# Graph passes: GpSimd's scratch memsets go, and a wait in mid-group comes in

## The chip, the cores and the metric

The kernel runs on one core of a Trainium2 chip. A core has TensorE (PE: matrix products; "PEld" are its weight loads), VectorE (DVE), ScalarE (ACT), GpSimd (POOL) and SyncE (SP, which here issues DMAs and posts semaphores). They run side by side and wait for each other by semaphores. The metric is the device time in microseconds (us) of one execution, as the median of several.

## What is computed

One graph of 6250 nodes (256 features each) and 206,250 edges sorted by destination is used twice:

```python
edge_index = jnp.stack([src, dst])
x = x + _L0_gnn_ref(_layernorm(x), edge_index, ...)   # graph attention, 4 heads: softmax over each node's edges, weighted sum of rows h[src]
x = x + _L0_ffn_ref(_layernorm(x)[None], ...)[0]      # 8 experts, top 2
x = x + _L1_gnn_ref(_layernorm(x), src, dst, edge_weight, ...)  # sum of edge_weight * row[src] per dst, then dense layers
x = x + _L1_ffn_ref(_layernorm(x)[None], ...)[0]      # attention on a second graph of 131,072 edges picks among 4 experts
```

The change touches the two passes over the 206,250 edges: "attention" (first line, tag g0) and "weighted" (third line, tag g1).

## The kernel before, in words

Both passes are built by `graph_pass`. Edges come in tiles of 128. A tile's source rows are fetched from a table in HBM by one indirect DMA of GpSimd (a gather, one row per partition). A one-hot matrix of the tile's destinations within a block of 128 nodes is made by VectorE, and TensorE multiplies the two: the product is the tile's sum per node, which VectorE adds to the block's row of `acc` in SBUF. There are 49 node blocks. A tile whose edges straddle two blocks is used once for each, so TensorE and VectorE go through `NS` = 1664 slots.

Eight tiles are a group (`GRP` = 8, `HG` = 4 is half of it), and the gathered rows lie in a ring of four groups (`RINGS` = 4). GpSimd's instructions run in order. Before each group it waits until the place in the ring is free.

Attention (`step_attending`, 208 groups k, gathers at L834): the wait ahead of group k is for TensorE's sums of group k-4 (`summed(k - RINGS, PAIRS - 1)` on the semaphore "part"). VectorE's step for a group needs all its 8 gathers (L996 is the first instruction that reads them), scales the rows (L990), and adds the sums of the group before (L953). TensorE's sums are L1124. From group 107 on VectorE also ranks the edges of the second graph (a scan L906 and a predicated copy L912 in every second group). After the last group GpSimd issues 16 scatters of that ranking (`tail`, L618).

Weighted (`step_placing`, 202 groups g of 8 gathers at L845, since each tile is fetched once): TensorE goes by 208 steps of 8 slots (L1156), each in two halves of 4 slots, and each half posts the semaphore "sum". VectorE adds them at L961 and makes the one-hots at L941. Because of the doubled tiles, TensorE's slot of a tile is later than the tile's own number by the number b of its node block (0 to 48). A step of TensorE waits until every group that it reads has landed whole (ScalarE posts that at L1050), so a step that reads the end of group g-2 and the start of group g-1 runs after the last gather of g-1 has landed. How far the sums are in terms of gathered groups comes from a table (`tables.summed(g)`): SyncE waits at L822 for the half that holds the last tile of group g and then raises the semaphore "room" by one. GpSimd waits ahead of group g for room of g - AHEAD + 1 with `AHEAD` = 3, which is the sums of group g-3. In the last 130 groups one scatter (L618) follows each group's gathers. A later pass over the second graph (tag q, gathers at L1699) has the same loop without memsets.

In both passes GpSimd clears a part of a scratch tile IDLE after every second gather (L838, L849). Nothing reads it.

Of the kernel before, what the change touches and what calls it, by code (L numbers as in the profile page):

```python
# [33 lines left out]
P = 128  # L34
# [20 lines left out]
TG = NTE // GRP  # L55
AHEAD = 3
# [90 lines left out]
def at_least(eng, sem, value):  # L147

    if not isinstance(value, int) or value > 0:
        eng.wait_ge(sem, value)  # L150
# [544 lines left out]
def graph_pass(sh, tag, planned, planned_block, table, width, acc, acc_zeroed, gather_done, rounds0, keep=None, gmax=None,  # L695
# [10 lines left out]
    RND = SG // RINGS  # L706
    HG = GRP // 2
    BANKS = 4
    names = ["loaded", "onehot", "added", "idle"]
    if attend:  # L710
        names += ["iota", "part", "copied", "z", "lr", "arg", "p", "pcol", "gp"]
    else:
# [3 lines left out]
    s = {n: sh.sem(f"{tag}_{n}") for n in names}  # L716
    with Scope(nc) as sc:
# [13 lines left out]
        WT = sc.sb(f"{tag}_WT", [P, NS]) if not attend else None  # L731
        G = sc.sb(f"{tag}_G", [P, RINGS, GRP, width])
        S = sc.sb(f"{tag}_S", [P, RINGS, GRP, P])
        IDLE = sc.sb(f"{tag}_IDLE", [P, HG, 32])
        if attend:
            pM = [sc.ps(f"{tag}_pM{j}", [P, 512]) for j in range(BANKS)]
        else:
# [1 line left out]
        if attend:  # L739
            ST = sc.sb(f"{tag}_ST", [P, GRP, P])  # L740
            PAIRS = GRP // 2
# [58 lines left out]
        def summed(k, pair):  # L800
            return k * PAIRS + 5 + pair
# [5 lines left out]
        @block.sync  # L807
        def _(sp):
            sp.dma_start(IDX[:, :], planned[0] if attend else src_tiles).then_inc(s["loaded"], 16)
            sp.dma_start(REL[:, :], planned[1]).then_inc(s["loaded"], 16)  # L810
            if attend:
                sp.dma_start(BLK[:, :], planned_block).then_inc(s["loaded"], 16)
            if ranking:
                sp.dma_start(DST, sort.dst_t).then_inc(s["loaded"], 16)
                sp.dma_start(SRC, sort.src_t).then_inc(s["loaded"], 16)
            if not attend:
                sp.dma_start(WT[:, :], planned[2]).then_inc(s["loaded"], 16)

                with sp.Fori(0, TG - AHEAD) as g:
                    sums = sp.value_load(tables.summed(g), min_val=1, max_val=2 * SG)  # L820
                    sp.wait_ge(s["sum"], sums)
                    sp.sem_inc(s["room"], 1)  # L822

        @block.gpsimd
        def _(pool):
            pool.wait_ge(s["loaded"], n_loads)

            def step_attending(k):

                r = k % RINGS  # L830
                if k >= RINGS:
                    pool.wait_ge(s["part"], summed(k - RINGS, PAIRS - 1))
                for u in range(GRP):
                    pool.indirect_dma_start(G[:, r, u, :], None, table, bass.IndirectOffsetOnAxis(  # L834
                        ap=IDX[:, k * GRP + u:k * GRP + u + 1].bitcast(U32), axis=0)).then_inc(gather_done[r], 16)
                    if u % 2 == 1:
                        at_least(pool, s["idle"], (k - 1) * HG + u // 2 + 1)
                        pool.memset(IDLE[:, u // 2, :], 0.0).then_inc(s["idle"], 1)  # L838

            def step_placing(g):  # L840

                r = g % RINGS
                at_least(pool, s["room"], g - AHEAD + 1)
                for u in range(GRP):
                    pool.indirect_dma_start(G[:, r, u, :], None, table, bass.IndirectOffsetOnAxis(  # L845
                        ap=IDX[:, g * GRP + u:g * GRP + u + 1].bitcast(U32), axis=0)).then_inc(gather_done[r], 16)
                    if u % 2 == 1:
                        at_least(pool, s["idle"], (g - 1) * HG + u // 2 + 1)
                        pool.memset(IDLE[:, u // 2, :], 0.0).then_inc(s["idle"], 1)  # L849
                if g >= TG - place:  # L850
                    sort.place(pool, 1)

            if attend:
                pool.iota(RANK, [[P, NTF]], base=P * NTS, channel_multiplier=1,
                          allow_small_or_imprecise_dtypes=True).then_inc(s["rank0"], 1)
                for k in range(SG):
                    step_attending(k)
                pool.wait_ge(s["prep"], 7)
                pool.wait_ge(s["addr"], 4)
                sort.place(pool, tail)  # L860
            else:
                for g in range(TG):
                    step_placing(g)
                sort.place(pool, tail)
# [1700 lines left out]
def build(nc, a, out):  # L2565
# [3 lines left out]
    with ExitStack() as ctx:  # L2569
# [23 lines left out]
        with Scope(nc) as layer:  # L2593
            keep = layer.sb("keep0", [P, NB, 2 * HEADS])
            gmax = layer.sb("gmax0", [P, HEADS])
            acc = layer.sb("acc0", [P, NB, D + HEADS])
            project_nodes(sh, "p0", stats, a["L0_gnn_W"], D + 2 * HEADS, att=(a["L0_gnn_att_src"], a["L0_gnn_att_dst"]),
                          table=table0, table_cols=D + HEADS, keep=keep, keep_from=D, zero=(acc, acc_zeroed[0]), clear=slots)
            table_maximum(sh, "m0", keep, 0, gmax)
            graph_pass(sh, "g0", planned, planned_block, table0, D + HEADS, acc, (acc_zeroed[0], NB), gather_done, 0,  # L2600
                       keep=keep, gmax=gmax, sort=sort, tail=16)
            finish_attention(sh, "f0", acc, table0, keep, gmax, a["L0_gnn_bias"], a["x"], sort, 60)
# [4 lines left out]
        with Scope(nc) as layer:  # L2607
            weights = layer.sb("weights0", [P, TOP, NB])
            pos = layer.sb("pos0", [P, TOP, NB], I32)
            pos_get = layer.sb("pos_get0", [P, TOP, NB], I32)  # L2610
            expert_of = layer.sb("expert_of0", [1, NT_MAX], I32)
            node_of = layer.sb("node_of0", [P, NT_MAX], I32)
            ew_scope = Scope(nc)
            ew = ExpertWeights(sh, ew_scope.__enter__(), "ew0", 8, 1024, a["L0_ffn_W1"], a["L0_ffn_b1"],
                               a["L0_ffn_W2"], a["L0_ffn_b2"], ln_g=a["L0_ffn_ln_g"], ln_b=a["L0_ffn_ln_b"])
            with Scope(nc) as inner:
                stats2 = inner.sb("stats2", [P, NB, 2])
                with Scope(nc) as router:
                    logits = router.sb("logits0", [P, NB, 8])
                    project_nodes(sh, "p1", stats, a["L0_ffn_Wr"], 8, keep=logits, stats2=stats2, sort=sort, count=37, fetch=ew.fetch)  # L2620
                    add_bias(sh, "rb", logits, a["L0_ffn_br"], 8)
                    second_stats(sh, "s2", stats2)
                    route(sh, "r0", 8, logits, weights, pos, pos_get, expert_of, sort, 20)
                order_rows(sh, "t0", 8, stats, stats2, pos, node_of, rows[0], ew, sort, 45)
            experts(sh, "e0", 8, 1024, ew, expert_of, node_of, rows[0], ys, y_stored, sort, 5)
            ew_scope.ctx.close()
            acc = layer.sb("acc1", [P, NB, D])
            tables = TileTables(sh, layer, "tt", planned_block, a["first_dst"], graph_rounds)
            combine(sh, "c0", weights, pos_get, ys, y_stored, (16 * ((tiles_of(8) + 1) // 2), 16 * (tiles_of(8) // 2)),
                    then=(stats, table1, acc, acc_zeroed[1], tables), sort=sort, scatters=10)  # L2630
            sh.end_layer()


            graph_pass(sh, "g1", planned, planned_block, table1, D, acc, (acc_zeroed[1], 1), gather_done, graph_rounds,
                       sort=sort, place=130, tail=8, src_tiles=a["src_t"], tables=tables)
            finish_weighted(sh, "f1", acc, stats, a["L1_gnn_W1t"], a["L1_gnn_W2t"], a["L1_gnn_b1"], a["L1_gnn_b2"], sort, 93)
# [84 lines left out]
```

## Time and profile before

| what | us |
|---|---|
| median of 3 runs (7681.4 to 7688.64) | 7682.64 |
| the profiled execution, its own time | 7684.64 |
| its span from first to last instruction | 7682.9 |
| GpSimd busy in the span | 5707.3 (74%) |
| TensorE busy | 5447.3 (71%) |
| VectorE busy | 3924.1 (51%) |
| ScalarE busy | 1568.1 (20%) |

The span is one line of time for the whole kernel. The attention pass lies at about 195 to 2344 us and the weighted pass at about 3650 to 5864 us. A busy share is a mean over all stages, so each stage is to be read by its own waits. Times of single instructions come from one profiled execution, a matmul's end is modelled, and a wait is put down to the event that came last before it ended.

### The profile page before, as it was taken

Reading aid. Unit: us, or ns where it says so; the run is one execution under the profiler, and the core shown is the slowest. Engines: PE = TensorE matmul, PEld = TensorE weight load, DVE = VectorE, ACT = ScalarE, POOL = GpSimd, SP = SyncE. Lnnn points to the kernel's source line nnn. Section 1 sums busy time; section 2 is a strip of 40 time slices with the busy share of each in tenths; the row PEclk is TensorE's granted clock in tenths of the full one; section 3 lists DMA queues with packets and bytes.
Section 4 is the critical chain, followed back from the end, with each engine's and each line's share of the span. In section 5 each row is a group of like instructions: output and inputs, shape, how many; then the busy total and the mean of one; then the engine's idle time right before and its main releaser. Section 6 shows DMA issues by size and latency. Waiting matters only on the chain. (4 is left out here: it accounts for less than half of the span.)

```text
span 7682.9 us, 117784 instructions
## 1 busy us (share of the span) xinstructions
PE 5447.3 (71%) x27644; PEld 4598.9 (60%) x27645; DVE 3924.1 (51%) x10109; ACT 1568.1 (20%) x3440; POOL 5707.3 (74%) x7330
## 2 busy tenths in 40 slices
PE   3888888777772599990555555555556589999993
PEld 3666666666661489880444434344435589999983
DVE  4777777888887500005454544444445533333326
ACT  1222222222220233330000000000001234444431
POOL 2888888888876577776888888888886577777762
PEclk7888888888885699995777777776777678888886
DMA  3333333333333255553333333333331133333698
GB/s 121 106 106 106 106 107 105 103 103 103 102 101 95 85 174 174 171 172 117 104 104 104 102 92 92 92 92 92 92 93 49 28 86 79 80 79 80 71 72 188
DMA packets 426071, 793.43 MB, mean 103 GB/s; under 512 B 129162, under 2 KB 267134, under 8 KB 425684
## 3 DMA queue, kind: packets, MB, share of 16 engines
q0 software_dynamic: 235504, 474.87, 26.8%
q1 hardware_dynamic: 190436, 317.20, 12.2%
q14 instruction: 97, 0.79, 0.0%
q8 instruction: 34, 0.56, 0.0%
HBM read 720.67 MB, written 70.98 MB: 103 GB/s over the span
## 5 line engine op out<-in xcount | busy, mean ns | idle before, releaser
L1156 PE MATMUL g_pM<-g_G,g_S 128*128 x3328 | 1196.6, 537 | 1190.0 <-ACTq L1050 1070.9
L834 POOL DMA_INDIRECT g_G<-table,X x1664 | 1611.4, 968 | 401.9 <-issue 385.6
L845 POOL DMA_INDIRECT g_G<-table,g_IDX x1616 | 1542.1, 954 | 416.7 <-issue 392.3
L1156 PEld LDWEIGHTS g_pM<-g_G,g_S 128*128 128x128 f32 x3328 | 916.0, 282 | 1470.5 <-issue 1272.4
L1124 PE MATMUL g_pM<-g_G,g_S 128*128 128x260 f32 x3328 | 1125.3, 481 | 407.5 <-DVE acc L953 400.6
L618 POOL DMA_INDIRECT slots<-sort_PAIR,sort_ADDR x1024 | 1029.1, 1005 | 415.4 <-issue 276.2
L1699 POOL DMA_INDIRECT q_G<-table,slot x1072 | 1028.3, 959 | 370.3 <-issue 320.6
L961 DVE TENSOR_TENSOR acc<-g_pM,acc 128x256 f32 x1664 | 698.4, 420 | 1005.4 <-PE g_pM L1156 1002.6
L1124 PEld LDWEIGHTS g_pM<-g_G,g_S 128*128 128x128 f32 x3328 | 706.5, 231 | 692.7 <-DVE acc L953 566.5
L953 DVE TENSOR_TENSOR acc<-g_pM,acc 128x260 f32 x1664 | 711.2, 427 | 188.8 <-PE g_pM L1124 40.4
L941 DVE TENSOR_SCALAR g_S<-iota,g_REL,g_WT 128x128 f32<-128x128 f32 x1664 | 591.2, 356 | 193.2 <-issue 172.4
L990 DVE TENSOR_TENSOR g_G<-g_G,g_pF 128x512 f32<-128x512 f32 x832 | 546.7, 678 | 0.3 <-ACT g_pF L1073 0.3
L1360 ACT ACTIVATE f_XT<-f_pT 128x512 f32<-128x512 f32 x49 | 28.8, 597 | 2329.2 <-PE f_pT L1373 2329.2
L1486 PE MATMUL q_pH<-ew_XT,ew_W 128*128 (+1 forms) x3136 | 489.3, 321 | 0.0
L1486 PEld LDWEIGHTS q_pH<-ew_XT,ew_W 128*128 128x128 f32 x3136 | 462.6, 232 | 3.3
L1114 PEld LDWEIGHTS g_pA<-keep,g_ST 128*128 128x128 f32 x3328 | 407.8, 197 | 78.3 <-issue 71.4
L2356 DVE TENSOR_TENSOR e_Y<-e_pY,ew_B 128x256 f32<-128x256 f32 x105 | 44.6, 425 | 797.5 <-PE e_pY L2387 797.5
L1735 DVE TENSOR_TENSOR q_Z<-q_G,q_pA 128x32 f32<-128x32 f32 x134 | 25.2, 188 | 800.5 <-DMA q_G<-table,slot 787.6
L1496 PE MATMUL q_pY<-ew_W,ew_GT 128*128 128x256 f32 x1568 | 426.8, 421 | 0.0
L1114 PE MATMUL g_pA<-keep,g_ST 128*128 x3328 | 410.9, 256 | 11.9 <-ACT g_ST L1057 1.2
L2378 PEld LDWEIGHTS e_pH<-e_XT,e_W 128*128 128x128 f32 x3360 | 393.3, 193 | 8.6 <-issue 3.3
L2387 PE MATMUL e_pY<-ew_W,e_GT 128*128 x1680 | 389.0, 385 | 12.8 <-issue 5.8
(336 smaller groups left out, 7382.3 us busy)
## 6 DMA issues: line engine op xcount, KB each, us to landing
e_W<-in_L_ffn_W SPq DMA_DIRECT2D x210, 512.0 KB, 4.4
sort_PAIR<-slot_rows SPq DMA_DIRECT2D x66, 512.0 KB, 4.5
g_G<-table,X POOLq DMA_INDIRECT x1664
g_G<-table,g_IDX POOLq DMA_INDIRECT x1616
ys_all<-ew_Y SPq DMA_DIRECT2D x196, 128.0 KB, 1.8
sm_Y<-ys_all SPq DMA_DIRECT2D x28, 896.0 KB, 10.6
q_ST<-slot_rows SPq DMA_DIRECT2D x34, 512.0 KB
sort_ADDR<-slot_rows SPq DMA_DIRECT2D x34, 512.0 KB
```

What stands on the lines that cost most here:

```text
L618: pool.indirect_dma_start(self.slots, bass.IndirectOffsetOnAxis(ap=self.ADDR[:, t:t + 1].bitcast(U32), axis=0), self.PAIR[:, t, :], None). ...
L834: pool.indirect_dma_start(G[:, r, u, :], None, table, bass.IndirectOffsetOnAxis(ap=IDX[:, k * GRP + u:k * GRP + u + 1].bitcast(U32), axis= ...
L845: pool.indirect_dma_start(G[:, r, u, :], None, table, bass.IndirectOffsetOnAxis(ap=IDX[:, g * GRP + u:g * GRP + u + 1].bitcast(U32), axis= ...
L941: v.tensor_scalar(S[:, r, u, :], sh.iota[:, :], rel, WT[:, bass.ds(k * GRP + u, 1)], ALU.is_equal, ALU.mult).then_inc(s["onehot"], 1)
L953: v.tensor_tensor(node_sums(blk), pM[u % BANKS][:, 0:width], node_sums(blk), ALU.add).then_inc(s["added"], 1)
L961: v.tensor_tensor(node_sums(blk), pM[r % 2 * 2 + u // HG][:, u % HG, :], node_sums(blk), ALU.add).then_inc(s["added"], 1)
L990: v.tensor_tensor(rows, rows, fac, ALU.mult).then_inc(s["gp"], 1)
L1114: m = pe.matmul(pA[:, r % 2, u, :], ST[:, u, :], nodes, start=True, stop=True)
L1124: m = pe.matmul(pM[u % BANKS][:, 0:width], S[:, r, u, :], G[:, r, u, :], start=True, stop=True)
L1156: m = pe.matmul(pM[r % 2 * 2 + half][:, u % HG, :], S[:, r, u, :], rows.rearrange("p a d -> p (a d)"), start=True, stop=True)
L1486: m = pe.matmul(self.pH[e % n][:, c, :], self.W1[:, e, k, c * P:(c + 1) * P], self.XT[:, bass.ds(i, 1), k, :].rearrange("p a m -> p (a m)" ...
L1699: pool.indirect_dma_start(G[:, r, u, :], None, table, bass.IndirectOffsetOnAxis(ap=node_of_slot[:, 2 * (k * GRP + u):2 * (k * GRP + u) + 1 ...
```

## The change

The scratch tile IDLE, its memsets and its semaphore go from both passes. In their place GpSimd gets one wait per group, ahead of its fifth gather: in the attention pass for the sums of group k-3 (from group 3 on), in the weighted pass for room of g - AHEAD + 2, which is the sums of group g-2 (from group 2 to the last but one). The waits ahead of the groups stay as they are.

```diff
-    names = ["loaded", "onehot", "added", "idle"]
+    names = ["loaded", "onehot", "added"]
-        IDLE = sc.sb(f"{tag}_IDLE", [P, HG, 32])
...
             def step_attending(k):
                 for u in range(GRP):
                     pool.indirect_dma_start(G[:, r, u, :], None, table, bass.IndirectOffsetOnAxis(
                         ap=IDX[:, k * GRP + u:k * GRP + u + 1].bitcast(U32), axis=0)).then_inc(gather_done[r], 16)
-                    if u % 2 == 1:
-                        at_least(pool, s["idle"], (k - 1) * HG + u // 2 + 1)
-                        pool.memset(IDLE[:, u // 2, :], 0.0).then_inc(s["idle"], 1)
+                    if u == HG - 1 and k >= AHEAD:
+                        pool.wait_ge(s["part"], summed(k - AHEAD, PAIRS - 1))
...
             def step_placing(g):
-                    if u % 2 == 1:
-                        at_least(pool, s["idle"], (g - 1) * HG + u // 2 + 1)
-                        pool.memset(IDLE[:, u // 2, :], 0.0).then_inc(s["idle"], 1)
+                    if u == HG - 1 and g < TG - 1:
+                        at_least(pool, s["room"], g - AHEAD + 2)
```

## Rows read from the trace of the kernel before

**Rows 1.** GpSimd's gathers in the later pass q (count | busy, mean ns | idle before, releasers):
```profile
L1699 POOL DMA_INDIRECT q_G<-table,slot x1072 | 1028.3, 959 | 370.3 <-issue 320.6 <-PE slot_sums L1798 40.1 <-POOLq L135 9.6
```

**Rows 2.** Waits in the weighted pass, 3651 to 5852: us in total, times, longest:
```profile
PE g_pM L1156 <- ACTq L1050: 1063.2, 171, 184.5
POOL g_G L845 <- issue: 392.3, 1582, 0.3
```

**Rows 3.** Ranking stage of attention; weighted groups 75 on: us, PE, PEld, DVE, ACT, POOL, PEclk, DMA, GB/s:
```profile
1266.00:2322.00 1056.00, 826.75 (x4008) 646.25 (x4007) 922.52 (x1806) 244.34 (x398) 855.07 (x1213) 0.86 0.37 102
4383.00:5852.00 1469.00, 767.49 (x2128) 587.61 (x2128) 662.79 (x2129) 0.00 (x0) 1187.24 (x1678) 0.74 0.32 92
```

**Rows 4.** Timeline of GpSimd, weighted group 109: start, us, instruction [idle before]:
```profile
4797.49 0.95 POOL L845 DMA_INDIRECT g_G<-table,g_IDX  x1 [0.17 <-issue]
4798.75 0.95 POOL L845 DMA_INDIRECT g_G<-table,g_IDX  x1 [0.30 <-issue]
4799.69 0.14 POOL L849 MEMSET g_IDLE<- 128x32 f32 x1
4800.00 0.95 POOL L845 DMA_INDIRECT g_G<-table,g_IDX  x1 [0.17 <-issue]
```

**Rows 5.** Timelines around a wait of GpSimd ahead of attention group 207:
```profile
2311.63 1.00 DVE L953 TENSOR_TENSOR acc<-g_pM,acc 128x260 f32 x2
...
2311.75 0.95 POOL L834 DMA_INDIRECT g_G<-table,X  x1 [3.44 <-PE g_pM L1124]
```

**Rows 6.** Timelines of weighted group 23: fifth gather, TensorE's step, second half's add:
```profile
3885.44 0.95 POOL L845 DMA_INDIRECT g_G<-table,g_IDX  x1 [0.16 <-issue]
...
3882.36 6.64 PE L1156 MATMUL g_pM<-g_G,g_S 128*128 x16 [3.54 <-DVE g_S L941]
...
3889.15 0.42 DVE L961 TENSOR_TENSOR acc<-g_pM,acc 128x256 f32 x1 [0.42 <-PE g_pM L1156]
```

**Rows 7.** Timelines of weighted group 16: fifth gather, first half's add:
```profile
3814.73 0.95 POOL L845 DMA_INDIRECT g_G<-table,g_IDX  x1 [0.17 <-issue]
...
3815.49 0.43 DVE L961 TENSOR_TENSOR acc<-g_pM,acc 128x256 f32 x1 [4.20 <-PE g_pM L1156]
```

**Rows 8.** Timelines of weighted group 30: fifth gather, TensorE's step:
```profile
3955.85 0.95 POOL L845 DMA_INDIRECT g_G<-table,g_IDX  x1 [0.17 <-issue]
...
3952.64 5.40 PE L1156 MATMUL g_pM<-g_G,g_S 128*128 x16 [4.53 <-ACTq L1050]
```

**Rows 9.** Timeline of VectorE, weighted group 109: first half's add:
```profile
4799.44 0.43 DVE L961 TENSOR_TENSOR acc<-g_pM,acc 128x256 f32 x1 [5.51 <-PE g_pM L1156]
```

**Rows 10.** Fifth gathers of weighted groups 160 and 161, TensorE's steps:
```profile
5380.81 0.98 POOL L845 DMA_INDIRECT g_G<-table,g_IDX  x1 [0.17 <-issue]
...
5392.19 1.02 POOL L845 DMA_INDIRECT g_G<-table,g_IDX  x1 [0.17 <-issue]
...
5376.44 5.43 PE L1156 MATMUL g_pM<-g_G,g_S 128*128 x16 [5.42 <-ACTq L1050]
5387.79 6.57 PE L1156 MATMUL g_pM<-g_G,g_S 128*128 x16 [5.92 <-ACTq L1050]
```

**Rows 11.** Attention: matmuls with group 57's last sum, fifth gather of group 60:
```profile
787.75 4.85 PE L1124 MATMUL g_pM<-g_G,g_S 128*128 128x260 f32 x12 [2.34 <-DVE acc L953]
...
799.54 0.95 POOL L834 DMA_INDIRECT g_G<-table,X  x1 [0.17 <-issue]
```

**Rows 12.** Attention, ranking: first gather of group 191, VectorE's read of group 190:
```profile
2139.72 0.95 POOL L834 DMA_INDIRECT g_G<-table,X  x1 [2.12 <-PE g_pM L1124]
...
2155.45 0.19 DVE L996 TENSOR_TENSOR g_Z<-g_G,g_pA 128x32 f32<-128x32 f32 x1
```

**Rows 13.** The attention pass's end: last tail scatter, group 207's read, last adds:
```profile
2340.79 0.96 POOL L618 DMA_INDIRECT slots<-sort_PAIR,sort_ADDR  x1 [0.31 <-issue]
...
2331.96 0.19 DVE L996 TENSOR_TENSOR g_Z<-g_G,g_pA 128x32 f32<-128x32 f32 x1 [1.51 <-PE g_pM L1124]
...
2342.43 1.00 DVE L953 TENSOR_TENSOR acc<-g_pM,acc 128x260 f32 x2 [0.21 <-PE g_pM L1124]
```

## The prediction

> **What bounds the kernel now.** I read the list of waits of the weighted pass first [rows 2]. GpSimd waited for nothing but its own issue: 392.3 us in 1582 gaps, 0.25 us each. TensorE stood 1063.2 us for ScalarE's report that a group had landed, so it follows the gathers. The weighted pass therefore ends when GpSimd has issued its 1616 gathers and its scatters, and each microsecond that GpSimd stands there is a microsecond of the kernel, unless something else is late. Then I read the attention pass in two stages. Until group 106 it is paced by the gathers as well. In the ranking stage VectorE is busy for 922.52 of 1056 us [rows 3] and GpSimd is found waiting for TensorE's sums ahead of groups [rows 5, 12]; the ring is full and VectorE's chain sets the pace.
>
> **The memsets.** 4 x (208 + 202) = 1640 memsets of 0.14 us go, 230 us of busy time by the sum. What counts is the time from gather to gather. With a memset between them it is 4800.00 - 4798.75 = 1.25 us, without one 4798.75 - 4797.49 = 1.26 us [rows 4]: the gap between two gathers is 0.30 us either way, and the memset lies inside it. The later pass, which has no memsets, has 320.6 us of such gaps for 1072 gathers, 0.30 us each, too [rows 1]. The bounds of the gain are thus 0 and 0.01 us for each of the 4 pairs of a group, over the 106 + 202 groups in which GpSimd sets the pace: 12 us. I take 6.
>
> **The wait in the weighted pass.** Ahead of its fifth gather, group g now waits for all sums of group g-2. Queued behind it are GpSimd's remaining four gathers, the scatter, and every later group; TensorE, and VectorE behind it, wait for those gathers. When are these sums done? Slots run behind tiles by the block number b. Where b mod 8 is 0, the step that ends group g-2 needs no rows of g-1 and has long run. In all other groups it needs group g-1 whole, so it can start only when the last gather of g-1, issued just before g begins, has landed. For b mod 8 of 1 to 4 the last tile is in the first half of that step, for 5 to 7 in the second. GpSimd reaches its fifth gather 5.0 us after the group's start. It is a race between 4 gathers and landing plus half a step or a whole one, and the rows show both runners.
>
> What GpSimd adds once the sum is there: TensorE's step of group 23 ended at 3882.36 + 6.64 = 3889.00 and VectorE's add, which waits for the same sum, began 0.15 later [rows 6]; a gather that waited for a sum began 0.12 after such an add [rows 5]. So the gather starts 0.27 us after the step's end or 0.12 after the add. SyncE's hop by way of "room" is in neither row; I take nothing for it, 0.1 as its bound. The stall of a group is this time less the fifth gather's start now:
> - first half, groups up to 74: 3815.49 + 0.12 - 3814.73 = 0.9 us [rows 7], for 35 groups;
> - second half, same stretch: 3889.00 + 0.27 - 3885.44 = 3.8 us [rows 6] and 3952.64 + 5.40 + 0.27 - 3955.85 = 2.5 us [rows 8], mean 3.15, for 24 groups;
> - first half, groups with a scatter between (which gives TensorE 1.3 us more): 4799.44 + 0.12 - 4800.00 = -0.4 us, no stall [rows 4, 9], for 65 groups;
> - second half, same stretch: 5376.44 + 5.43 + 0.27 - 5380.81 = 1.3 us and 5387.79 + 6.57 + 0.27 - 5392.19 = 2.4 us [rows 10], mean 1.9, for 48 groups.
>
> The rest has b mod 8 of 0 or lies at the ends. Sum: 31 + 76 + 0 + 91 = 198 us. The same subtraction done for each of the 199 waiting groups gives 190 us, with 105 groups late; I take 190. A stall is not made up in the next group: the sum of g-2 hangs on the last gather of g-1, which moves with the stall, so each late group pays anew. No group is early enough to give it back, since GpSimd has no other idle time there. SyncE's, VectorE's and ScalarE's work shifts with it.
>
> The unknown is TensorE's pace in the step. Its 16 matmuls take 5.40 us in one step and 6.64 in another [rows 6, 8], at a mean granted clock of 0.74 of 2.4 GHz over the stretch [rows 3], between the levels of 1.2 and 2.4 GHz. If all second halves ended as the early ones above, the stalls would be 35 x 0.9 + 24 x 2.5 + 48 x 1.3 = 154 us; if as the late ones, 31 + 24 x 3.8 + 48 x 2.4 = 237 us. These are the ends of this term.
>
> The Trainium skill has a rule that speaks for the far end (TensorE: Matmul & The Clock Gate, "Loop structure matters more than you think"): with a long DMA wait between matmuls "PE goes cold". By it the stalls, which lengthen TensorE's own idle time, would raise the sum from 190 to 237 us. The trace agrees so far as steps at both paces stand there with 3.5 to 5.9 us of idle before them [rows 6, 8, 10], and does not say which of the two longer gaps will bring.
>
> **The wait in the attention pass.** Up to group 106 it is met early: the matmuls with group 57's last sum ended by 787.75 + 4.85 = 792.60, and group 60 reached its fifth gather at 799.54 [rows 11], 7 us later. Cost nothing; the cover is that margin. In the ranking stage the wait does bind: the sum that released group 191 at 2139.72 will now hold group 190 in its middle, and its last gather ends at 2139.72 + 3 x 1.25 + 0.95 = 2144.4 instead of 2137.5. VectorE reads that group at 2155.45 [rows 12], 11 us later, so nothing is late behind it. At the end of the pass something is. The sum that released group 207 at 2311.75 [rows 5] now releases the fifth gather of 206, and 207 starts 4 x 1.25 = 5.0 us later. Its last gather ends near 2326.5, before VectorE's read at 2331.96, but the 16 tail scatters end at 2340.79 + 0.96 + 5.0 = 2346.8 where VectorE's last add ends at 2343.4 [rows 13]. The pass ends 3 us later (0 to 5).
>
> **Sum.** +190 + 3 - 6 = +187 us. Against the profiled execution's own 7684.64 us that is 7871.6; its time is 2.0 above the median of 7682.64, so I predict 7870 us for the median.
>
> **Rivals.**
> - *Every step slow.* TensorE runs each step at its slow pace, as the clock falls in the longer gaps. Stalls 237 us or more; the 65 scatter groups have only 0.4 us of margin, and another 0.4 us each would add 26. Time 7917 to 7945. For it: the steps of 6.57 and 6.64 us. Against: steps of 5.40 us after 4.5 us of idle.
> - *A stall bought once per stretch.* If TensorE, given more time, needed the newer group less often, only the first group of a stretch would stall, and the cost would shrink towards 40 to 110 us, 7720 to 7790. Against it: which rows a step needs is fixed by the edges, not by time.
> - *Wait met already, no change.* The count is off by one group from my reading, or SyncE posts earlier than the half's end. Then only -6 + 3 us are left, 7680. Against it: SyncE's loop waits for the very half that holds the last tile.
> - *Faster.* The memset costs its 0.14 us on GpSimd after all, so that the gap without one falls to 0.17, the value seen after a memset [rows 4]. Then 1640 x 0.14 = 230 us come back, and with 190 + 3 us of stalls the kernel is 37 us faster: 7646. It decides from a gap of 0.19 us downwards. Against it: gaps of 0.30 us wherever no memset stands [rows 1, 4].
>
> **How the numbers follow.** Chances: forecast 0.81, every step slow 0.08, stall once 0.05, wait met 0.03, faster 0.03. Low end 7682.64 + 154 + 0 - 12 = 7825; high end 7682.64 + 237 + 5 + 0 = 7925, and 0.1 us for SyncE in 107 groups would add 11: 7935. I set the low end at 7820 for matmuls that start sooner after landing. About 0.2% (15 us) is what a measurement of this kernel can tell from no change. Faster 0.03, same 0.03, slower 0.94.
>
> **What would show it.** In the profile after, GpSimd's gathers L845 should wait some 190 us on SyncE or TensorE in about 105 groups, none in the four or five groups around each wrap of b mod 8; the weighted pass should be longer by that, and the attention pass by under 5 us. Gather to gather should stay at 1.25 us. It would be wrong if that distance fell below 1.2 us, if the late groups were not those of the second halves, or if a stage behind the passes changed its length.

## The result, and the profile after

The changed kernel takes 7900.18 us (median, 7896.91 to 7903.07), the kernel before 7682.02 beside it: 1.0286 times as long, 95% interval 1.0273 to 1.0299. That is 218 us more, where 187 were forecast (7870 us, range 7820 to 7935). One execution of the study, of the kernel with only the memsets out, took 16119 us; no ratio counts it, and without it that kernel's median is 7671.30 us.

From the page of the changed kernel, its span, its busy times and GpSimd's gathers of the weighted pass (L843):

```profile
span 7896.1 us, 116142 instructions
PE 5483.0 (69%) x27644; PEld 4620.9 (59%) x27645; DVE 3918.4 (50%) x10109; ACT 1568.3 (20%) x3440; POOL 5456.9 (69%) x5690
L843 POOL DMA_INDIRECT g_G<-table,g_IDX x1616 | 1534.3, 949 | 744.2 <-issue 459.4
```

GpSimd is busy 250 us less and the span is 213 us longer: its memsets went, and it now stands and waits. The list of waits of the weighted pass, 3651 to 6080 us (us in total, times, longest), says for whom (L821 is SyncE's posting of "room", L1047 ScalarE's report that a group has landed):

```profile
PE g_pM L1153 <- ACTq L1047: 1290.6, 188, 183.1
POOL g_G L843 <- issue: 458.8, 1506, 0.3
POOL g_G L843 <- SPq L821: 264.4, 107, 4.0
```

The last row is new; in [rows 2] GpSimd waited for issue alone. There were 107 such waits. Each holds the 0.305 us gap that every gather has, so the stalls are 264.4 - 107 x 0.305 = 231.8 us. TensorE's wait for landed groups grew as well, from 1063.2 to 1290.6 us: who waits for the gathers waits longer.

The timelines of groups 23 and 161 (GpSimd's fifth gather, TensorE's step), which answer to [rows 6] and [rows 10]:

```profile
3897.95 6.14 PE L1153 MATMUL g_pM<-g_G,g_S 128*128 x16 [7.26 <-ACTq L1047]
3904.40 0.94 POOL L843 DMA_INDIRECT g_G<-table,g_IDX  x1 [3.68 <-SPq L821]
...
5569.88 6.44 PE L1153 MATMUL g_pM<-g_G,g_S 128*128 x16 [7.19 <-ACTq L1047]
5583.50 6.46 PE L1153 MATMUL g_pM<-g_G,g_S 128*128 x16 [7.18 <-ACTq L1047]
```

(A step is 8 matmuls of the program; the profile records each of them twice, as x16.) Group 23's gather starts 0.31 us after the step's end at 3904.09. TensorE stands idle for 7.2 us before each of these steps, and they last 6.1 to 6.5 us; from step to step it is 13.62 us in the later stretch, where it was 11.35 [rows 10]. The steps of the later second halves last 6.46 us in the mean, near the slow one of [rows 10], where they took 5.94 before. The granted clock tells the same (busy time by stretch; the columns are those of [rows 3]), for the whole pass, for a stretch whose groups do not stall and for one whose groups do:

```profile
3651.00:6080.00 2429.00, 1253.03 (x3320) 956.66 (x3321) 1033.10 (x3311) 0.00 (x0) 1664.90 (x1748) 0.69 0.31 87
4497.00:4667.00 170.00, 87.11 (x240) 66.75 (x240) 75.33 (x241) 0.00 (x0) 128.92 (x135) 0.74 0.33 93
4668.00:4831.00 163.00, 80.37 (x200) 61.28 (x201) 59.98 (x192) 0.00 (x0) 102.29 (x109) 0.63 0.27 77
```

Stall by stall, from the gaps ahead of the fifth gathers:

| groups | forecast, us each | measured, us each | number | measured sum |
|---|---|---|---|---|
| first halves, no scatter | 0.9 | 0.92 | 35 | 32 |
| second halves, no scatter | 3.15 | 3.60 | 24 | 86 |
| first halves, with scatter | none | none | 65 | 0 |
| second halves, with scatter | 1.9 | 2.35 | 48 | 113 |

The weighted pass's first to last gather took 221.8 us longer than before; that of the attention pass 3.2 us. The rest of the span lost 11.8 us in stages whose code is the same. Of those the later gather pass (tag q) accounts for 9.5. The prediction named a change of a stage behind the passes as a sign of being wrong. But with its code untouched this pass was also 3.5 us shorter in the trace with only the memsets out and 11.2 us shorter in that of the control below, so I read no cause into it.

### The profile page after: what moved, and what is told of

Read it like the earlier page. It is cut to its first block and busy times, and to the rows that moved or that the text cites. A ratio compares the mean times of both kernels' runs of the same rounds, so it can differ in the third digit from the quotient of the medians.

```text
span 7896.1 us, 116142 instructions
## 1 busy us (share of the span) xinstructions
PE 5483.0 (69%) x27644; PEld 4620.9 (59%) x27645; DVE 3918.4 (50%) x10109; ACT 1568.3 (20%) x3440; POOL 5456.9 (69%) x5690
## 5 line engine op out<-in xcount | busy, mean ns | idle before, releaser
L1153 PE MATMUL g_pM<-g_G,g_S 128*128 x3328 | 1255.4, 558 | 1351.0 <-ACTq L1047 1290.6
L843 POOL DMA_INDIRECT g_G<-table,g_IDX x1616 | 1534.3, 949 | 744.2 <-issue 459.4
L1153 PEld LDWEIGHTS g_pM<-g_G,g_S 128*128 128x128 f32 x3328 | 958.4, 295 | 1648.0 <-issue 1433.4
L1121 PEld LDWEIGHTS g_pM<-g_G,g_S 128*128 128x128 f32 x3328 | 698.0, 228 | 706.3 <-DVE acc L950 581.3
L938 DVE TENSOR_SCALAR g_S<-iota,g_REL,g_WT 128x128 f32<-128x128 f32 x1664 | 574.9, 346 | 191.3 <-issue 172.5
```

Source lines behind the costliest of these rows:

```text
L938: v.tensor_scalar(S[:, r, u, :], sh.iota[:, :], rel, WT[:, bass.ds(k * GRP + u, 1)], ALU.is_equal, ALU.mult).then_inc(s["onehot"], 1)
L1121: m = pe.matmul(pM[u % BANKS][:, 0:width], S[:, r, u, :], G[:, r, u, :], start=True, stop=True)
L1153: m = pe.matmul(pM[r % 2 * 2 + half][:, u % HG, :], S[:, r, u, :], rows.rearrange("p a d -> p (a d)"), start=True, stop=True)
```

## The experiments

Every kernel below leaves the reference's computation whole. Times are medians; a ratio is to the kernel before on the same chip.

**Only the memsets out.** The changed kernel without its two waits:

```diff
-                    if u == HG - 1 and k >= AHEAD:
-                        pool.wait_ge(s["part"], summed(k - AHEAD, PAIRS - 1))
...
-                    if u == HG - 1 and g < TG - 1:
-                        at_least(pool, s["room"], g - AHEAD + 2)
```

> The memsets go, no wait comes in. My theory (the memset lies in the 0.30 us between two gathers): 0 to 12 us faster than before, 7670 to 7682 us; gather to gather 1.25 us all through the weighted pass. Rival (a memset costs its own 0.14 us on GpSimd): 1640 of them would give 230 us back, near 7450 us.

Measured: 7672.06 against 7679.52 us, 0.9990 times (0.9980 to 0.9999), 7.5 us faster. Its gathers (count | busy, mean ns | idle before):

```profile
L841 POOL DMA_INDIRECT g_G<-table,g_IDX x1616 | 1542.5, 954 | 512.8 <-issue 492.4 <-DMA g_WT<-planned 20.4
```

The idle time ahead of a gather is 492.4 us where it was 392.3 with memsets in half of the gaps [rows 2]: 808 memsets of 0.145 us, 117 us, left this pass, and 100 us of idle time took their place. That settles the rival by which 230 us would come back. In the traces 1.1 us lie between first and last gather of the weighted pass, 3.3 between those of the attention pass and 3.5 in the later gather pass, whose code is the same. So the 7.5 us can't all be put down to the memsets. This kernel's median is the lowest of the study.

**Only the weighted pass's wait**, memsets and attention pass as before:

```diff
                         pool.memset(IDLE[:, u // 2, :], 0.0).then_inc(s["idle"], 1)
+                    if u == HG - 1 and g < TG - 1:
+                        at_least(pool, s["room"], g - AHEAD + 2)
```

> The kernel before with only the weighted pass's wait ahead of the fifth gather; memsets stay, the attention pass is as before. My theory: this wait is the whole loss, so 225 to 240 us slower than before, 7907 to 7922 us, that is the 7900 of the changed kernel plus what the memsets' removal gave. Rival (the attention pass's wait carries a part): clearly less than 215 us slower.

Measured: 7902.01 us, 1.0291 times (1.0275 to 1.0306), 222 us slower, with the same 107 waits. Its stalls are 222 us, and this wait alone makes the whole loss. The time is 5 us below the range that I expected, whose lower end, 225, is inside the interval of 211 to 235 us.

**Only the attention pass's wait**, memsets and weighted pass as before:

```diff
                         pool.memset(IDLE[:, u // 2, :], 0.0).then_inc(s["idle"], 1)
+                    if u == HG - 1 and k >= AHEAD:
+                        pool.wait_ge(s["part"], summed(k - AHEAD, PAIRS - 1))
```

> The kernel before with only the attention pass's wait; memsets stay, the weighted pass is as before. My theory: the wait binds in the last third of the pass, where VectorE sets the pace, and costs nothing there; at the end of the pass up to 5 us by the later tail scatters: 7680 to 7688 us. Rival (a stall of GpSimd shows in full): the 23 us that the changed kernel's trace has at this wait, 7705 us.

Measured: 7680.89 us, 1.0000 times (0.9991 to 1.0010). The list of waits of its ranking stage, 1266 to 2330 us:

```profile
POOL g_G L834 <- PE g_pM L1126: 23.3, 43, 3.4
```

The time shows nothing, to within 7 us. It is a weak test, though: the kernel before has 14.8 us in 23 such waits in the same stage, so the new wait added only 8.5. That a stall is free behind VectorE's pace is seen better in the traces: VectorE's last add ended 2150.8 us after the pass's first gather in the kernel before and 2150.9 in the changed kernel, though the first gather of group 207 came 3.2 us later. In the trace of this run it ended 3.2 us later, at 2154.0; that execution was the slowest of its ten, 7696.02 us.

**The wait at another gather.** The same sums, waited for ahead of the fourth, the sixth or the seventh gather instead of the fifth:

```diff
-                    if u == HG - 1 and g < TG - 1:
+                    if u == HG - 2 and g < TG - 1:     # fourth; HG: sixth; HG + 1: seventh
                         at_least(pool, s["room"], g - AHEAD + 2)
```

> The changed kernel with the weighted pass's wait two gathers later, ahead of the seventh gather; it waits for the same sums. My theory (a race between gathers issued and landing plus half a step or a whole one): each stall is 2.5 us shorter. First halves 1.0 - 2.5 and the second halves of the later groups 2.35 - 2.5 vanish, the 24 early second halves keep 3.6 - 2.5 = 1.1 us: 17 to 30 us in all, time 7690 to 7705 us. Rival (GpSimd pays something for each wait that it meets, wherever it stands): over 7780 us.

> The changed kernel with the weighted pass's wait one gather earlier, ahead of the fourth gather. My theory: each margin shrinks by 1.25 us, so 35 first halves stall 2.2 us, 24 early second halves 4.85, 48 late second halves 3.6, and the 65 first halves that had 0.4 us to spare now stall 0.8: 77 + 116 + 173 + 52 = 418 us, time 8070 to 8110 us. Rival (only the groups that stall now stall, the others are not near): 366 us, 8040 us.

> The changed kernel with the weighted pass's wait one gather later, ahead of the sixth. With the wait at the fourth and at the fifth gather the second-half groups settled at the same 13.65 us each, with steps of 5.2 and 6.45 us. My reading: a group that waits lasts 2.2 us (landing) + TensorE's step + 0.3 us (answer) + the gathers behind the wait, 4.7 us for four of them. With three behind it (3.45 us) that is 5.95 us + step. For 13.65 us a step would have to last 7.7 us, longer than any seen (6.7), so the groups must leave that rhythm: 11.1 to 12.7 us each with steps of 5.1 to 6.7, which is stalls of 1.0 to 2.6 us in the 24 early second halves and 0 to 1.3 us in the 48 late ones, none in first halves; 50 to 100 us in all, time 7720 to 7775 us. Rival (the 13.65 us are a fixed rhythm of the loop, wherever the wait stands): stalls of 3.6 and 2.35 us stay, 200 us, 7870 us.

| wait ahead of | time, us | ratio (interval) | stalls in the trace, us | groups that stall |
|---|---|---|---|---|
| fourth | 8011.03 | 1.0428 (1.0410 to 1.0445) | 339 | 172 |
| fifth (the change) | 7900.18 | 1.0286 (1.0273 to 1.0299) | 232 | 107 |
| sixth | 7758.28 | 1.0101 (1.0084 to 1.0118) | 83 | 55 |
| seventh | 7684.66 | 1.0015 (0.9999 to 1.0031) | 8 | 15 |

(The last column counts stalls over 0.1 us.) The race is shown: move the wait by a gather and the groups that lose it are others. At the fourth the 65 scatter groups with 0.4 us of margin stall 0.86 us each, as expected, and 172 groups are all but those that wrap (b mod 8 of 0). What a wait costs without a stall is too little to see: at the seventh 199 waits stand, and the time lies 12.6 us over that of the kernel with only the memsets out, of which 8 are stalls; the rest is less than the interval can tell.

Two expectations missed. At the fourth I had 418 us and a time of 8070 to 8110, and the stalls are 339; at the seventh 17 to 30 us and they are 8. Both had added or taken 1.25 us per gather and left TensorE's steps as they were. At the fourth the first halves (2.15 us) and the scatter groups came out as expected, and the whole miss lies in the 72 second halves: 208 us where 289 were expected. The timelines of an early second-half stretch show the steps change. Wait at the fourth gather (TensorE's step, the released gathers):

```profile
4409.73 5.21 PE L1153 MATMUL g_pM<-g_G,g_S 128*128 x16 [8.42 <-ACTq L1047]
4415.24 0.94 POOL L843 DMA_INDIRECT g_G<-table,g_IDX  x1 [3.91 <-SPq L821]
```

Wait at the fifth, the changed kernel:

```profile
4327.40 6.45 PE L1153 MATMUL g_pM<-g_G,g_S 128*128 x16 [7.22 <-ACTq L1047]
4334.16 0.94 POOL L843 DMA_INDIRECT g_G<-table,g_IDX  x1 [3.98 <-SPq L821]
```

Wait at the sixth:

```profile
4230.44 5.38 PE L1153 MATMUL g_pM<-g_G,g_S 128*128 x16 [4.78 <-ACTq L1047]
4241.80 6.51 PE L1153 MATMUL g_pM<-g_G,g_S 128*128 x16 [5.98 <-ACTq L1047]
4254.30 5.40 PE L1153 MATMUL g_pM<-g_G,g_S 128*128 x16 [5.99 <-ACTq L1047]
```

Once the wait binds, gathers, landing and step of one group stand in a row: 2.2 us from the last gather's end to the step, the step, 0.3 us to the next gather, then the gathers behind the wait. With five, four and three of them (5.95, 4.7 and 3.45 us) that is 2.2 + 5.2 + 0.3 + 5.95 = 13.65, 2.2 + 6.45 + 0.3 + 4.7 = 13.65, and 2.2 + 5.4 or 6.5 + 0.3 + 3.45 = 11.35 or 12.45 us; the groups' starts in the traces lie 13.7, 13.65, and by turns 11.4 and 12.5 us apart. The sixth came out as expected in the time, the sum and the early second halves (1.3 to 2.5 us); of the late ones a few stalled 2.0 to 2.3 us, where 1.3 was the most that I expected. The rival, a fixed rhythm of 13.65 us wherever the wait stands, fell. The sum says how landing, step and gathers add up to a group's length. Why steps of 5.2 and 6.45 us make it the same twice isn't known.

The clock changes as well. The stretch with groups 56 to 66, wait at the fourth (columns of [rows 3]):

```profile
4339.00:4500.00 161.00, 65.52 (x208) 50.84 (x208) 63.89 (x207) 0.00 (x0) 90.73 (x97) 0.77 0.27 78
```

TensorE stood longer before each step there than in the changed kernel, 8.4 us against 7.2, and the granted clock was higher: 0.77, where the changed kernel has 0.63 over its groups 55 to 66 (4270 to 4430 us) and over the stretch shown above.

**TensorE kept busy.** In each step of the weighted pass TensorE does 12 or 24 more matmuls while it would stand waiting for the gathers. They write a bank that the step overwrites, and wait until VectorE has read it:

```diff
                 at = places(k)
+                at_least(pe, s["added"], (k - 2) * GRP + HG)
+                for _ in range(24):      # 12 in busy_tensor_12
+                    pe.matmul(pM[r % 2 * 2][:, 0, 0:P], sh.ones[:, :], sh.ident[:, :], start=True, stop=True)
                 pe.wait_ge(s["tiles"], k + 1)
```

> The changed kernel, and in each step of the weighted pass TensorE does 12 more matmuls of 128 columns into a PSUM bank that the step overwrites, while it would stand waiting for the gathers. Their results are not used. Theory A (the stalls are as long as they are because the steps run at the lower clock after the long idle time): the steps shorten from some 6.4 us towards 3.7 to 5, the stalls of the first halves (1 us) go and those of the second halves fall from 3.6 and 2.35 by 1 to 2.7 us, the sum from 232 to 20 to 130 us, time 7690 to 7800 us. Theory B (landing and fixed times make the stall, the pace of the matmuls is no matter): 7895 to 7910 us.

Measured with 12: 7878.06 us, 1.0259 times (1.0243 to 1.0274), stalls 202 us in 84 groups. That is in neither theory's range. In its trace two kinds of group are seen (steps L1156):

```profile
4007.67 6.38 PE L1156 MATMUL g_pM<-g_G,g_S 128*128 x16 [4.63 <-ACTq L1047]
...
4044.96 3.72 PE L1156 MATMUL g_pM<-g_G,g_S 128*128 x16 [1.97 <-ACTq L1047]
```

After 4.6 us of idle time this step takes 6.4 us, after 2 us 3.7. Twelve matmuls were too few to fill the idle time of the groups that stall most. Hence the same with 24, and as a control the kernel before with 24:

> As busy_tensor_12 with 24 added matmuls a step. There the first halves' stalls went in most groups where TensorE's idle time fell to 2 us (steps of 3.7 us), but the second halves kept 4.5 us of idle, steps of 6.4 us and their stalls. Theory A (pace after idle time): with 24 the idle time of those groups falls under 2 us as well, their steps go to 3.7 us, and stalls of 0.9 us in 24 groups and none in the later ones are left: 20 to 60 us in all, time 7690 to 7735 us. Theory B (the second halves' stalls do not hang on the pace): some 190 us of stalls stay, 7870 us.

> Control: the kernel before with the same 24 added matmuls a step in the weighted pass. GpSimd sets the pace there and no wait binds, so shorter steps give nothing: within 10 us of before. If it is over 10 us faster, the added matmuls help in some other way and busy_tensor_24 is to be read against it; if slower, they are in TensorE's way.

Measured with 24: 7736.46 us, 1.0071 times (1.0054 to 1.0087), stalls 66 us in 51 groups. The control: 7680.22 us, 0.9996 times (0.9986 to 1.0005). The whole pass's busy time and clock with 24 in the changed kernel:

```profile
3651.00:5926.00 2275.00, 1969.10 (x13296) 1822.35 (x13296) 1042.10 (x3320) 0.00 (x0) 1670.23 (x1748) 0.96 0.33 94
```

The same of the control:

```profile
3651.00:5864.00 2213.00, 1947.77 (x13307) 1809.07 (x13308) 1043.39 (x3321) 0.00 (x0) 1791.81 (x2560) 0.97 0.34 96
```

The granted clock rose from 0.69 to 0.96 of 2.4 GHz, and 164 us of the 218 came back, though TensorE had more to do. In the kernel before the same clock gave nothing, as no wait hung on a step. The 66 us of stalls and the time of 7736 us lie just over the expected 60 and 7735: some steps still took 5.4 us, in a timeline of the 24:

```profile
4241.61 5.40 PE L1156 MATMUL g_pM<-g_G,g_S 128*128 x16 [1.86 <-ACTq L1047]
4254.16 3.71 PE L1156 MATMUL g_pM<-g_G,g_S 128*128 x16 [1.78 <-ACTq L1047]
```

Idle time alone doesn't tell which: 1.86 us stand before the slow one, 1.78 before the fast one. That stays open.

## Why the prediction was right, and where it was off

**What bounds the pass.** Right. Every stall came out as time: 232 us of stalls, 222 us of the weighted pass, 222 us when this wait stood alone. And all along the series with the wait moved, the time less that of the kernel with only the memsets out is near the stalls: 8011 - 7672 = 339 us against 339, 7900 - 7672 = 228 against 232, 7758 - 7672 = 86 against 83, 7685 - 7672 = 13 against 8. In the changed kernel's attention pass, where VectorE sets the pace of the ranking stage, its last add came no later.

**The memsets.** Right that they cost next to nothing: 6 us were taken, the runs show 7.5 (interval about 1 to 15), too coarse to confirm the 6. The reason given, that they lie inside the gap between two gathers, is shown by the idle time that took their place.

**The race in the weighted pass.** Right in which groups stall (those with b mod 8 of 1 to 4 only where no scatter stands between; 5 to 7 everywhere; 0 nowhere), in their number (107 waits; 107 forecast by classes, 105 group by group), and in the answer time: 0.27 us with SyncE's hop unknown, 0.31 measured, so the hop costs 0.04, 4 us in all. First halves were forecast at 0.9 and took 0.92 us.

**The term that was mis-sized: the second halves.** The prediction took TensorE's steps as they were in the trace before, some fast and some slow, and made it 190 us with 154 and 237 as ends. The stalls came to 232, next to the far end. The step that failed is "I take 190": it kept the steps' old lengths. In the groups that stall in their second halves, the steps that the trace shows whole (62 of the 72) had taken 5.95 us in the mean (5.1 to 6.8). Now they took 6.43: 0.44 us more in the early 24 groups and 0.52 in the late 48. Over the 72 that is 36 us of the 42; SyncE's hop is 3 more. TensorE's idle time ahead of these steps had been 3.5 to 5.9 us [rows 6, 8, 10], and with the stalls it was 7.2. That a step's length sets the stall is shown: with 24 added matmuls most steps took 3.7 us, and 166 of the 232 us went. That the longer idle time made the steps slow is argued from the two traces, and no run isolates it. The rule of the Trainium skill that the prediction weighed (TensorE: Matmul & The Clock Gate, "Loop structure matters more than you think") spoke for the far end of 237 us, and here the measured 232 agrees with it against my choice.

Longer idle time doesn't always mean a slower step, though. With the wait at the fourth gather TensorE stood even longer, 8.4 us, its steps were shorter, 5.2 us, and the granted clock was higher, 0.77 against 0.63. In the trace before, too, 6.64 us followed 3.54 us of idle time and 5.40 us followed 4.53 [rows 6, 8]. So something besides the idle time ahead of it sets a step's length, and by which law these runs don't settle.

**The time is nearer than its terms.** The stalls came out 42 us over the 190. With 232 in its place the prediction's own sum gives 229 us, and 218 were measured. The weighted pass lost 10 us less than its stalls, 8 of them as its gathers were shorter (1534.3 us busy against 1542.1), and the stages with unchanged code gave 12 back. Neither was forecast, and that the miss is 31 us and not 42 is luck.

**The end of the attention pass.** Forecast +3 us, measured +3.2, but not by the way forecast. The prediction had the last gather and the tail scatters 5.0 us later, and let VectorE's last add, which ended after the scatters before, take 2 us of that. From the changed kernel's timeline, GpSimd's first instruction behind the tail scatters, the last of which ended at 2341.91 + 0.96 = 2342.87:

```profile
2347.74 0.95 POOL L618 DMA_INDIRECT slots<-sort_PAIR,sort_ADDR  x1 [4.88 <-PEq L135]
```

The same 4.88 us stand there in the kernel before, where the add ended 1.7 us after the last scatter; here it ended 1.5 us before it. So it was the scatters that counted in both, and all of their delay came through. The delay itself was 3.2 us and not 5.0, since the awaited sum came 1.8 us sooner than in the trace before, counted from the pass's first gather. Two errors cancelled. Counted the same way, this next instruction came at 2156.0 to 2161.3 us in the seven traces with the attention wait and at 2151.4 to 2154.0 in the four without, so the wait costs some 4 us (an estimate, the mean difference).

**The rivals.** "Every step slow" had the right mechanism for the second halves and was too high as a time, 7917 to 7945: the 65 scatter groups kept their margin, which takes the upper part of it away, and the measured time lies under 7917 for the 10 and 12 us named above. "A stall bought once per stretch" fell: all 12 groups of each late stretch stall alike. "Wait met already" and "faster" fell with the 107 waits on SyncE and with the run without memsets. The price of "faster" was set too high, too: its 230 us count all 1640 memsets, and the 308 groups in which GpSimd sets the pace hold 1232, 172 us at 0.14, which would not have outweighed 193 us of stalls.

## What to carry to other kernels

A wait on the engine that sets the pace is free only while what it waits for is done earlier; work out that margin instruction by instruction, and look whether the awaited work itself hangs on what the engine has just issued, since then a stall comes back in every round. Here 2.5 us of margin, two gathers, were the difference between 0.2% and 2.9%. And do not carry the duration of the awaited work over from the trace before: TensorE's steps took 3.7 to 6.8 us for the same matmuls, and a new stall changes when they start and how long TensorE has stood idle.

## What the runs showed of the hardware

- The same step (x16 in the profile) mostly took 3.7 us where the mean granted clock was 0.96 to 0.97 of 2.4 GHz, and 6.3 to 6.5 us in a stretch at 0.63; the levels are 1.2 and 2.4 GHz, and these are means over a stretch. Longer idle time did not always go with a lower clock: 0.63 with 7.2 us of idle time before each step, 0.77 with 8.4.
- With the wait ahead of the fourth and of the fifth gather the stalling groups settled at the same 13.65 us, with steps of 5.2 and 6.45 us; with it ahead of the sixth they took 11.4 and 12.5 us by turns. Why isn't known.
- Filling TensorE's idle time with 24 more matmuls beside the 8 of a step, whose results nobody reads, made a kernel whose wait binds 2% faster (7900 to 7736 us), and one without such a wait no faster (7680 against 7680 us).
- A memset of 0.14 us between two indirect DMAs on GpSimd cost nothing that the time between gathers shows: 1.25 us with it, 1.26 without [rows 4], and 1.25 in the changed kernel, which has none.
- A gather of the weighted pass took 949 to 953 ns in the mean in the six traces with both edits (949 in the changed kernel) and 954 to 957 in the five others. Over 1616 gathers 5 ns are 8 us, most of the 10 by which the weighted pass grew less than its stalls. Why it takes both edits isn't known.
